# Low parts of split weights on VectorE or GpSimd, and transposes that wait for all scans of a unit

## The reference

```python
proj = hidden_states @ W_in.T                       # H=1024 -> 2*2048
u, gate = jnp.split(proj, 2, axis=-1)
u = silu(causal_conv4(u) + conv_b)
dt, Bm, Cm = jnp.split(u @ Wx.T, [64, 80], axis=-1) # then an RMS norm of each
delta = softplus(dt @ Wdt.T + dt_bias)
def step(state, xs):                                # 512 steps, D=2048, N=16
    dA = jnp.exp(d_t[..., None] * A)
    state = dA * state + (d_t * u_t)[..., None] * B_t[:, None, :]
    y_t = jnp.einsum('bdn,bn->bd', state, C_t)
y = (y + u * D_param) * silu(gate)
x = layernorm(x + y @ W_out.T)
x = layernorm(x + x @ W.T + b + low_rank_by_route(x))
```

## Time and profile before

| what | value |
|---|---|
| three runs | 2257.61, 2262.97, 2263.51 us (median 2262.97) |
| span of the profiled execution | 2257.2 us |
| busy, PE / DVE / ACT / POOL | 2063.3 / 1986.4 / 1486.3 / 1824.8 us |
| scans on VectorE | 1024, mean 1203 ns |
| drives on GpSimd | 255 of full size, mean 4581 ns |
| low parts of weights on GpSimd | 128 of 128x512, mean 1291 ns |

### The profile page before, as it was taken

One profiled execution on the slowest core, in us unless ns is written; L12 is line 12 of the kernel. 1 busy time (PEld: TensorE's weight loads), 2 busy tenths in 40 slices (PEclk: granted clock), 3 DMA queues, 4 the chain that ended last, 5 costly groups with the idle time before them and its releaser, 6 DMA issues. The chain is left out here.

```text
span 2257.2 us, 30761 instructions
## 1 busy us (share of the span) xinstructions
PE 2063.3 (91%) x10528; PEld 1562.5 (69%) x10528; DVE 1986.4 (88%) x2398; ACT 1486.3 (66%) x2198; POOL 1824.8 (81%) x786
## 2 busy tenths in 40 slices
PE   8989789889999799799998997989999998897998
PEld 6867577778565478687875555867875556785677
DVE  4447779999999999899999999999999999999943
ACT  4478658787666677666886657676786667756531
POOL 4279899998898889768799997979788998698840
PEclk9989899999999999999999998999999999998999
DMA  4466566665333447655463432475463337443340
GB/s 157 138 223 235 204 221 219 203 205 179 92 118 86 126 132 239 209 193 182 158 199 95 111 96 96 147 264 171 143 203 101 110 96 233 148 144 132 101 143 38
DMA packets 168764, 354.84 MB, mean 157 GB/s; under 512 B 18656, under 2 KB 45408, under 8 KB 168608
## 3 DMA queue, kind: packets, MB, share of 16 engines
q1 hardware_dynamic: 168608, 352.87, 48.6%
HBM read 283.96 MB, written 68.85 MB: 156 GB/s over the span
## 5 line engine op out<-in xcount | busy, mean ns | idle before, releaser
L1563 POOL TENSOR_TENSOR drive<-delta_u,b_bcast 128x2048 f32<-128x2048 f32 (+1 forms) x257 | 1172.5, 4564 | 129.1 <-PE state_t L933 120.6
L1115 DVE TENSOR_TENSOR_SCAN drive<-decay,drive 128x512 f32<-128x512 f32 x1024 | 1190.5, 1203 | 62.0 <-POOL drive L1563 37.9
L1355 ACT ACTIVATE decay<-delta,a_sb 128x512 f32<-128x512 f32 x1024 | 694.7, 688 | 377.9 <-DVE drive L1115 374.6
L933 PEld LDWEIGHTS state_t<-identity,drive 128*128 128x128 f32 x4096 | 492.0, 146 | 311.1 <-DVE drive L1115 141.8
L933 PE MATMUL state_t<-identity,drive 128*128 128x128 f32 x4096 | 591.1, 284 | 119.8 <-DVE drive L1115 95.1
L1123 DVE SCALAR_TENSOR_TENSOR y_acc<-state_t,c_rows,y_acc 128x512 f32<-128x512 f32 x727 | 515.3, 734 | 54.3 <-PE state_t L933 51.7
L964 PE MATMUL bank<-cols_high,w_split 128*128 128x512 f32 (+1 forms) x1240 | 524.4, 423 | 26.6 <-POOL w_split L1588 11.8
L966 PE MATMUL bank<-cols_high,w_split 128*128 128x512 f32 (+1 forms) x1240 | 491.8, 397 | 0.0
L965 PE MATMUL bank<-cols_low,w_split 128*128 128x512 f32 (+1 forms) x1240 | 489.6, 395 | 0.0
L987 PE MATMUL bank<-channels,w_raw 128*128 128x512 f32 x896 | 420.2, 596 | 2.3 <-DVE rows L1177 2.0
L1568 POOL TENSOR_TENSOR y_acc<-y_acc,scaled 128x512 f32<-128x512 f32 x233 | 300.1, 1288 | 102.2 <-ACT scaled L1375 101.9
(11 more groups left out here) (204 smaller groups left out, 1451.8 us busy)
## 6 DMA issues: line engine op xcount, KB each, us to landing
w_split<-w_split SPq DMA_DIRECT2D x272, 512.0 KB, 4.0
b_bcast<-b_rows SPq DMA_DIRECT2D x256, 256.0 KB, 3.4
w_raw<-in_w_out SPq DMA_DIRECT2D x112, 256.0 KB, 3.0
w_raw<-in_w_in SPq DMA_DIRECT2D x96, 256.0 KB, 4.1
gates<-scratch SPq DMA_DIRECT2D x64, 256.0 KB, 3.7
scratch<-gates SPq DMA_DIRECT2D x64, 256.0 KB, 4.7
rows<-in_x_rows SPq DMA_DIRECT2D x4, 2048.0 KB, 8.2
out<-rows SPq DMA_DIRECT2D x16, 512.0 KB, 4.8
```

The costliest lines, as they stand in the source:

```text
L933: last = engine.transpose(bank[0:tile.shape[1], i * P:(i + 1) * P], tile, identity[:, :])
L1115: engine.tensor_tensor_scan(state, decay[(GT * s + t) % DECAYS][:, :], state, 0.0, ALU.mult, ALU.add).then_inc(signal["scan"])
L1355: engine.activation(decay[i % DECAYS][:, :], delta[:, g % 2, t, :], ACT.Exp, scale=a_sb[:, j, n:n + 1]).then_inc(signal["decay"])
L1563: engine.tensor_tensor(drive[key % DRIVES][:, tiles, :], du[:, tiles, :], row, ALU.mult).then_inc(signal[stage])
```

## The change

The rest of a split weight now has two ways, as the additions into `y_acc` had: `w_low` on GpSimd as before, or `w_rest`, the same subtraction on VectorE. The planner takes whichever engine is free first when the high part is there. In its table `w_rest` of a full tile lasts 0.75 us and `w_low` 1.23 us. The small rests of W_dt stay on VectorE (`dt_rest`). A transposition now has all four scans of its unit among its needs, where it had the fourth alone, and waits for each. A drive also has the drive before it as a need.

```diff
@@ Plan
+    def one_of(self, left, right):
+        self.rival[left], self.rival[right] = (right, 1), (left, 1)
@@ split_weight
-        put("POOL" if pool == "split" else "DVE", due - 3, 0.23 + part if pool == "split" else 0.35, rest, w, [("w_high", w)], give=[("raw", w)])
+        if pool == "split":
+            put("POOL", due - 3, 0.23 + part, "w_low", w, [("w_high", w)], give=[("raw", w)])
+            put("DVE", due - 3, 0.1 + 0.65 * part, "w_rest", w, [("w_high", w)], give=[("raw", w)])
+            plan.one_of(("w_low", w), ("w_rest", w))
+        else:
+            put("DVE", due - 3, 0.35, "dt_rest", w, [("w_high", w)], give=[("raw", w)])
@@ make_plan, the units
-        put("POOL", q - 8, 4.56 if s else 2.35, "drive", s, [("fetch", s), ("du", (b, g, 1))] + ([] if s else [("drive_begun", 0)]) + (
+        put("POOL", q - 8, 4.56 if s else 2.35, "drive", s, [("fetch", s), ("du", (b, g, 1)), ("drive", s - 1) if s else ("drive_begun", 0)] + (
-            put("PE", i + 4 - TURN_FIRST, 0.45, "turn", (s, tt), [("scan", (s, GT - 1)), *([] if i else [("ssm_norm", 0)])] + (
+            put("PE", i + 4 - TURN_FIRST, 0.45, "turn", (s, tt), [*[("scan", (s, t)) for t in range(GT)], *([] if i else [("ssm_norm", 0)])] + (
@@ tensor
-                    e.wait_ge(*done("scan", (s, GT - 1)))
+                    for t in range(GT):
+                        e.wait_ge(*done("scan", (s, t)))
@@ vector
+                elif stage == "w_rest":
+                    pair, cols = slot(key), WK * cols_of(key[0][0])[0]
+                    e.wait_ge(*done("w_high", key))
+                    engine.tensor_tensor(pair[:, 1, 0:cols], raw[place["raw", key]][:, 0:cols], pair[:, 0, 0:cols].bitcast(F32),
+                                         ALU.subtract).then_inc(signal["w_rest"])
```

More of the change, by code:

```diff
@@ L31, in pool_of, with rest_of @@
     return "dt" if DT_TILE <= tile < TILES else "split"
[L34 to L36 removed]
+def rest_of(w):
+    return [("dt_rest", w)] if DT_TILE <= w[0][0] < TILES else [("w_low", w), ("w_rest", w)]
 def low_of(b, k):
@@ L155, in arrange @@
             for what in piece["give"]:
-                to_give[what] = to_give.get(what, 0) + 1
+                to_give[what] = to_give.get(what, 0) + (name[0] != "w_rest")
         queues = {pool: sorted((p["due"], p["order"]) for p in self.pieces.values() if any(x == pool for x, _ in p["take"]))
@@ L162, in arrange @@
         at = {e: 0.0 for e in ENGINES}
-        now, dma, ends, finished, wanted, table = 0.0, 0.0, [], 0, len(self.pieces), None
+        now, dma, ends, finished, wanted, table, lost_ways = 0.0, 0.0, [], 0, len(self.pieces), None, set()
         for name, piece in self.pieces.items():
@@ L180, in arrange @@
                         wanted -= pieces
+                        lost_ways.add(lost)
                         for other in ENGINES:
@@ L214, in arrange @@
                     left[follower] -= 1
-                    if left[follower] == 0:
+                    if left[follower] == 0 and follower not in lost_ways:
                         piece = self.pieces[follower]
@@ L245, in split_weight @@
             return w, ("w_load", w)
[L246 removed]
+        part, rest = 1.0 if what[0] < ROUTE_TILE or what[0] >= TILES else 0.5, any_of(rest_of(w))
         put("SP", due - 6, 0.35, "raw_load", ("w", w), take=[("raw", w)], kb=256 * part)
         put("ACT", due - 4, 0.13 + 0.4 * part, "w_high", w, [("raw_load", ("w", w))], take=[(pool, w)])
[L249 removed]
+        if pool == "split":
[4 more added lines that the diff above has]
+            put("DVE", due - 3, 0.35, "dt_rest", w, [("w_high", w)], give=[("raw", w)])
         if n == keep:
[L251 to L252 removed]
+            put("SP", due, 0.35, "w_store", w, [rest], give=[(pool, w)], kb=512 if pool == "split" else 128)
+        return w, rest
     def split_ahead(what, due):
@@ L770, in in_sum, with rests @@
             return done(*plan.done_way(summed(s, tt)))
+        def rests(w):
+            return done(*plan.done_way(any_of(rest_of(w))))
         def x_first(k):
@@ L850, in _ @@
                     pair = slot(key)
-                    e.wait_ge(*done(rest_of(key[0][0]), key))
+                    e.wait_ge(*rests(key))
                     cols, planes = cols_of(key[0][0])
@@ L955, in _ @@
                     w = slot_of[stage, (b, j, k | (WK - 1))]
-                    e.wait_ge(*done("w_low" if w[1] <= kept_at[w[0]] else "w_load", w))
+                    e.wait_ge(*(rests(w) if w[1] <= kept_at[w[0]] else done("w_load", w)))
                     high, low = (k_tiles(slot(w)[:, i, :], cols) for i in range(2))
@@ L1048, in _ @@
                     high, low = (y[:, tt * P:(tt + 1) * P] for y in (y_high_of(k), y_rest[:, k, :]))
-                    e.wait_ge(*done("w_low", w))
+                    e.wait_ge(*rests(w))
                     e.wait_ge(*done(*y_low_of(k)))
```

## The result

The changed kernel takes 2324.95 us (median of 4 runs, 2315.8 to 2330.4) against 2263.24 us before: ratio 1.0276, 95% interval 1.0249 to 1.0304. The direction was forecast. The size was not: +62 us where +21 was predicted, outside the range up to 2304. The profiled execution has a span of 2314.0 us, 56.8 us above before's. Its own time of 2315.8 us is the lowest of the four runs.

What follows compares the result with a forecast made beforehand. VectorE was taken to set the pace from unit 16 on, GpSimd's queue before; -1 - 3 + 14.4 + 15.4 - 6 + 1 = +20.8 us gave a median of 2284 us, range 2248 to 2304.

Steps and rivals of the forecast that it cites:

- What bounds the kernel: VectorE sets the pace from 297 us to the last scan, 96% busy; in units 0 to 15 GpSimd's queue is tightest.
- The lock: On VectorE, a rest with two SBUF inputs waits until GpSimd's running instruction ends, then does its 0.69 us of work.
- The high bound: Between scans, a rest waits for the remainder of whatever GpSimd runs, even a whole drive of 4.58 us; taken for the forecast.
- The mean waits: Per rest on VectorE: 1.38 us in units 0 to 15, 1.54 in 16 to 47, 1.50 in 80 to 95.
- The low bound: Between scans, rests wait behind short GpSimd instructions only, not drives: 0.23 to 0.26 us a rest on the mean.
- rival A: Between scans, a drive does not hold VectorE, only short waits remain: -12 us, 2251 us; chance 0.25.
- Units 0 to 15: 142 to 297 us: GpSimd's relief saves 6.3 us, VectorE becomes fully filled; -3 us, between -14 and +10.
- Idle time taken up in units 16 to 47 and 80 to 95: Half of VectorE's idle time absorbs added work: 6.4 and 2.1 us, leaving +14.4 and +15.4 us.
- rival B: VectorE's idle time is hand-overs and gives nothing back, so high ends hold: +45 us, 2308 us; chance 0.12.
- Units 96 to 254: 14 additions leave VectorE and return as sums on GpSimd, which has room: -6 us, between -8 and -3.
- the four waits: On TensorE ahead of transpositions: no order changes, at most one added waiting instruction a unit; +1 us, 0 to 5.
- holds already: 0: The drive's new need for the drive before it is already met, so it costs 0 us.

Runs made afterwards that it cites:

- e1: Changed kernel, same order, but the 39 rests between scans on VectorE take their second input from PSUM instead of SBUF: 2281.69 us, ratio 1.0088 to before.
- e10: Kernel before, same order, but the 77 rests between drives on GpSimd subtract only 8 columns: 2258.23 us, ratio 0.9983 to before.
- e3: Changed kernel, same order, but the 39 rests between scans are 8 columns wide and take their second input from PSUM: 2269.13 us, ratio 1.0037 to before.
- e4: Changed kernel with no rest moved to VectorE, only the new needs of transpositions and drives, replanned: 2265.20 us, ratio 1.0025 to before.
- e9: Kernel before with only the drive's need for the drive before it, replanned, one wait per transposition: 2258.26 us, ratio 0.9984 to before.
- e6: Kernel before with 27 rests moved to VectorE, only before the first scan and behind the last: 2256.39 us, ratio 0.9976 to before.
- e5: Kernel before, same order, with one edit: transpositions wait for all four scans: 2267.59 us, ratio 1.0030 to before.
- e11: Changed kernel, same order, all 71 rests, but a transposition waits for the fourth scan alone: 2324.38 us, ratio 1.0282 to before.
- e7: Changed kernel, same order, with drives of units 1 to 47 and 80 to 95 split into two GpSimd instructions: 2305.32 us, ratio 1.0195 to before.

## Why the prediction was wrong

**What bounds the kernel**: right from unit 16 on, where e1 gives back 11.7 of 14.7 and 17.0 of 18.2 us that the rests wait. Wrong for units 0 to 15: 30.7 us less of GpSimd's work are worth 6.6 us there and 3.0 us in all (e10), not the reserve that I made of it.

**The lock**: right in kind and size. The high bound holds for a drive, 0.55 us behind its end. The mean waits were put at 1.38, 1.54 and 1.50 us, and measured 1.08, 1.34 and 2.02; in all 56.6 us predicted and 53.5 measured. The low bound and with it rival A fall: e1, in which no rest waits for GpSimd at all, is a little more than A would have been, and the changed kernel is 43 us above it. And even so e1 is 22 us slower than before, where A had 12 us faster: what was counted against the lock did not come even without the lock. The rule of the Trainium skill (SBUF — State Buffer, section Who interferes with whom) on two SBUF inputs held in e1 as well, where one input from PSUM was enough to end the waiting (677 ns a rest).

**The step that failed** is what I set against the lock: the idle time of VectorE and the relief of GpSimd that were to take up part of it. The first three of the four terms below miss by 21.5, 11.0 and 3.9 us, together as much as lies between the predicted +20.8 and the measured +56.8 us of span.

- Units 0 to 15, predicted -3 us, measured +18.5. I compared VectorE's work (148.6 us) with the stretch's length (148.7) as if the engine could be full. Its idle time there is made of hand-overs with TensorE and GpSimd and did not go: it is 32.1 us (173.6 - 141.5) after, 42.8 us before. Of the 29.3 us that VectorE is busy longer, 10.7 were taken from idle time and 18.5 came on top. The 6.3 us that GpSimd's relief was to bring did not come either: with no lock and hardly any work of the rests (e3) the stretch is 5.0 us longer than before.
- Idle time taken up in units 16 to 47 and 80 to 95, predicted 6.4 and 2.1 us. Busy time of VectorE grew by 18.2 and 22.2 us, the stretches by 16.9 and 23.9: given back were 1.3 and -1.7 us. In these two stretches rival B's mechanism was right, that nothing is given back; its +20.8 us were too much for the first, where the waits were shorter, and its +17.5 too little for the second. There the rests met drives 7 times in 9, and e4, in which no rest moved, already takes 139.7 us, 4.2 more than before.
- Units 96 to 254, predicted -6 us, measured -2.1. By the traces the drive's need alone brings what I predicted (e9, 1207.2 us against 1214.0 before), and the four waits, put at +1 us, take most of it again (e4, 1211.8; the changed kernel, 1211.9). This rests on single traces, and two of the same order differ by 1.9 us here (e6 has 1215.8). The gain is not where the additions left either: ten of them fewer in units 192 to 254 did not shorten these, since units 224 to 239 grew from 124.9 to 132.6 us in the changed kernel and to 130.7 in e9. The drive's need, which I had at "holds already: 0", arranged 20 additions anew, and in e9 gains 3.0 us over the whole.
- The median. The changed kernel's lies 10.9 us above its profiled span, before's 6.0 us. 5 of the 62 us are this. The mean clock granted to TensorE, as a share of full speed, was 0.957 in the changed kernel's profiled run and 0.950 to 0.951 in the other three.

**Small terms**: the four waits were put at +1 us, up to 5; alone they are about +6 (e5); what they cost in the changed kernel e11 does not tell. Before the first scan -1 us, measured 0.0, and behind the last 0, measured -0.5. The rests outside the units gain 5 us if they come alone (e6).

Split up by the runs against the kernel before: lock 43.3 (e1), work of the rests 12.6 (e1 to e3) and e3's remainder 9.6 us make 65.5. The changed kernel measured 61.7, against runs of before that were 3.7 us slower than those beside e1 to e3. The three are differences of neighbours in one row of kernels, so that they add up is no proof of each.

## What to carry to other kernels

Before work moves from GpSimd to VectorE, look where its inputs lie. Here a subtraction with two inputs in SBUF waited for the end of the GpSimd instruction that was running, itself one with two inputs in SBUF, so such work is to be priced by GpSimd's longest instruction, and belongs where GpSimd rests or has short ones. On an engine that is 96% busy, do not count its idle time as a reserve; what is made of hand-overs stays. And a need that seems to hold already can still rearrange a planned order: compare the orders for each edit by itself.

## What the runs showed of the hardware

- A rest usually gets in at the end of the GpSimd instruction that it waits for, but one and the same rest was kept waiting over several without a gap in four traces, up to 9.35 us over six (e7).
- 267 more waiting instructions of 51 ns each on TensorE cost about 6 us in a kernel in which VectorE is the busier engine in most stretches (e5).
